# Two-stream cross-attention on one core: one subtraction moved behind two maxima, four weight subtractions moved to GpSimd

## Chip, cores and metric

One core of one Trainium2 chip runs the whole kernel. The metric is the device time of that core in microseconds. In this document "us" is always microseconds, PE is TensorE (matmuls), DVE is VectorE, ACT is ScalarE, POOL is GpSimd and SP is SyncE, which only issues transfers.

## The reference

A cross-attention layer: 2 x 2048 tokens of 640 channels attend, in 20 heads of 32, to 77 context vectors each (the second, image part of the context is empty here), and the input is added back.

```python
q = _split_heads(hidden_states @ Wq.T, H)
k = _split_heads(text @ Wk.T, H)
v = _split_heads(text @ Wv.T, H)
out_text = _merge_heads(_attend(q, k, v, sm_scale))   # softmax(q k * sm_scale) v
out = out_text + IP_SCALE * out_ip
out = out @ Wo.T + bo
return out + residual
```

## The kernel before

**Tiles.** The 4096 tokens are cut into NB = 8 blocks `t` of 512, the 640 channels into G = 5 groups `g` of 128, and each group holds 4 heads. The unit of work is a step (t, g), forty in all. Every engine runs its own program over the same steps, in its own fixed order: `run(engine, step, ...)` calls `step(t, g)` for all of them, the middle blocks in a hardware loop. The engines meet only at semaphores.

**Precision.** Each operand of a large product is split in two: a rounded high part (`x_hi`, `wq_hi`, `p_hi`, `attn_hi`) and the low rest (`x_lo`, ...). Three matmuls (hi·hi, lo·hi, hi·lo) make one product. The high part is an ACT copy or exponential. The low part is a subtraction of two tensors in SBUF, and these subtractions are divided between DVE and POOL: of the five chunks of x and of attn DVE has chunks 1 and 3 (`DVE_CHUNKS`), POOL 0, 2 and 4; of the four heads' probabilities DVE has head 0, POOL 1, 2 and 3.

**A step on PE** (`step`, L828): `values` of the step before (ps_pv, ps_den, L729 and L734), scores of heads 0 and 1 (ps_s, L722), `max_scores` tiles 0 and 1 of the next step (ps_m, L708), two chunks of an output projection (ps_o, L676), `max_scores` 2 and 3, scores 2, two more chunks, scores 3, `transpose_max` (ps_m, L713), the last chunk, and the query projection `project_q` of the step after the next (ps_q, L676, fifteen matmuls). `max_scores` has two buffers, so tiles 2 and 3 wait for DVE's maxima 0 and 1 (`max_done`, L704); `transpose_max` waits for all four (L712). `values` waits for `norm_done` (L740), the `normalise` that DVE made in the step before.

**A step on DVE** (`step`, L592): in the steps where x is split, `x_low` of chunk 1; then the maxima 0 and 1 (L534), `p_low` of head 0 (L541), the maxima 2 and 3, `x_low` of chunk 3, `invert_den` (two transposes and a reciprocal, L547 to L551), `normalise` (L561), `finish_out` (L580), and, once ACT has rounded q, `q_low` (L527).

**A step on POOL** (L341): `x_low` of chunks 0 and 2, `p_low` of head 1, `x_low` of chunk 4, `p_low` of heads 2 and 3. **On ACT** (L447): `x_high` of chunks 0 to 2, the two exponentials (p_f, p_hi) of heads 0 and 1, `x_high` of 3 and 4, heads 2 and 3 with `copy_max` between them, then `q_high`.

**Where x is split.** `x_split_at` gives block t + 1 at g = 3 of the blocks t = 1 to 6, so six steps of the forty split x. In this trace they lie one in every 50 us; block 0 and block 1 of x are split elsewhere.

**Start-up.** Until step (1, 0) PE runs `fill`, which also makes v (`project_v`, `transpose_v`). In it ACT rounds and DVE subtracts one chunk of wq a step (`query_group`: chunks 1 to 4 in the steps (-1, 3), (-1, 4), (0, 0), (0, 1)), each behind `q_high` and `q_low` of its step. Chunk 0 is made ahead of the steps. wo is rounded by ACT and subtracted by POOL (`wo_low`), its chunks 0 and 1 at the end of step (0, 1).

Of the kernel before, what the change touches and what calls it, by code (L numbers as in the profile page):

```python
# [18 lines left out]
def xattn_kernel(nc, x, ctx, wq, wk, wv, wo, bo, out):  # L19
# [63 lines left out]
    def query_group(t, g):  # L83

        return (nth(t, g) + 3,) if isinstance(t, int) and -2 <= nth(t, g) < G - 3 else ()
# [54 lines left out]
    with ExitStack() as stack:  # L140
# [159 lines left out]
        @block.gpsimd  # L300
        def _(pool):
            nc.gpsimd.memset(ident[:, :], 0.0).then_inc(zero_done, 1)
            pool.wait_ge(zero_done, 1)
            nc.gpsimd.affine_select(out=ident[:, :], in_=ident[:, :], compare_op=ALU.not_equal, fill=1.0,
                                    base=0, pattern=[[-1, P]], channel_multiplier=1).then_inc(ident_done, 1)
            pool.wait_ge(ident_done, 1)
            nc.gpsimd.memset(k_packed[:, :, :, :].bitcast(F32), -1.0).then_inc(const_done, 1)
            pool.wait_ge(const_done, 1)
            for i in range(RS):
                nc.gpsimd.memset(q_packed[:, i, :, :].bitcast(F32), 0.0).then_inc(q_cleared, 1)  # L310
            nc.gpsimd.memset(ones[:, :], 1.0).then_inc(const_done, 1)

            def x_low(t, chunks):
                for c in chunks:
                    pool.wait_ge(xhi_done, G * t + c + 1)
                    nc.gpsimd.tensor_tensor(x_lo[:, c, :], x_f[:, c, :], x_hi[:, c, :].bitcast(F32),  # L316
                                            ALU.subtract).then_inc(xlo_pool, 1)

            def p_low(t, g, i):

                pool.wait_ge(phi_done, HG * nth(t, g) + i + 1)
                pool.wait_ge(pf_done, HG * nth(t, g) + i + 1)
                if exists(shift(t, g, -1)[0]):
                    pool.wait_ge(pv_done, nth(t, g))
                nc.gpsimd.tensor_tensor(p_lo[:, i, :], p_f[:, i, :], p_hi[:, i, :],  # L325
                                        ALU.subtract).then_inc(plo_pool, 1)

            def attn_low(t, chunks):
                for c in chunks:
                    pool.wait_ge(ahi_done, G * t + c + 1)  # L330
                    nc.gpsimd.tensor_tensor(attn_lo[:, c, :], attn[:, c, :], attn_hi[:, c, :].bitcast(F32),
                                            ALU.subtract).then_inc(alo_pool, 1)

            x_low(0, POOL_CHUNKS)

            def wo_low(c):
                pool.wait_ge(wo_hi_done, c + 1)
                nc.gpsimd.tensor_tensor(wo_lo[:, c, :], wo_sb[:, c, :], wo_hi[:, c, :].bitcast(F32),
                                        ALU.subtract).then_inc(wo_lo_done, 1)

            def step(t, g):  # L341
                xt, (at, chunks) = x_split_at(t, g), attn_split_at(t, g)
                mine = [c for c in POOL_CHUNKS if c in chunks]
                if xt is not None:
                    x_low(xt, POOL_CHUNKS[:2])
                if exists(t):
                    p_low(t, g, 1)
                if xt is not None:
                    x_low(xt, POOL_CHUNKS[2:])
                attn_low(at, mine[:1])  # L350
                if exists(t):
                    p_low(t, g, 2)
                    p_low(t, g, 3)
                attn_low(at, mine[1:])
                if isinstance(t, int) and (t, g) == (0, 2):
                    x_low(1, POOL_CHUNKS)
                for c in wo_chunks(*shift(t, g, -1)):
                    wo_low(c)

            run(pool, step, *LOOP)  # L360

        @block.scalar
        def _(act):
# [12 lines left out]
            def diagonal_k(b, heads):  # L376
                act.wait_ge(mask_done, 1)
                act.wait_ge(khi_done, G)
                for i in heads:
                    nc.scalar.mul(k_diag[:, :, b, L * i:L * (i + 1)],  # L380
                                  k_hi[:, :, L * b:L * (b + 1)].bitcast(F32),
                                  head_mask[:, i:i + 1]).then_inc(diag_done, 1)

            def w_high(w_in, w_sb, w_hi, done, chunks):
                for c in chunks:
                    act.wait_ge(w_in[c], 16)
                    nc.scalar.copy(w_hi[:, c, :], w_sb[:, c, :]).then_inc(done, 1)
# [55 lines left out]
            x_high(0, range(G))  # L443
            start_k()
            diagonal_k(0, range(HG))

            def step(t, g):  # L447
                xt, (at, chunks) = x_split_at(t, g), attn_split_at(t, g)
                if xt is not None:
                    x_high(xt, range(0, 3))  # L450
                if exists(t):
                    exponentials(t, g, 0)
                    exponentials(t, g, 1)
                for tile in out_tiles(*shift(t, g, -1)):
                    store(*tile)
                if xt is not None:
                    x_high(xt, range(3, G))
                attn_high(at, [c for c in (0, 1) if c in chunks])
                if exists(t):
                    exponentials(t, g, 2)  # L460
                for v in value_group(t, g):
                    v_high(v)
                if exists(shift(t, g, 1)[0]):
                    copy_max(*shift(t, g, 1))
                if exists(t):
                    exponentials(t, g, 3)
                attn_high(at, [c for c in (2, 3) if c in chunks])
                for tile in out_tiles(*shift(t, g, 1)):
                    load_residual(*tile)
                attn_high(at, [c for c in (4,) if c in chunks])  # L470
                if exists(shift(t, g, 2)[0]):
                    q_high(*shift(t, g, 2))
                if isinstance(t, int) and (t, g) == (0, 2):
                    x_high(1, range(G))
                w_high(wq_in, wq_sb, wq_hi, wq_hi_done, query_group(t, g))
                if isinstance(t, int) and t == 0 and g <= 1:
                    diagonal_k(1, range(HG // 2 * g, HG // 2 * (g + 1)))
                w_high(wo_in, wo_sb, wo_hi, wo_hi_done, wo_chunks(*shift(t, g, -1)))
# [9 lines left out]
        def _(dve):  # L488
# [30 lines left out]
            def x_low(t, chunks):  # L519
                for c in chunks:  # L520
                    dve.wait_ge(xhi_done, G * t + c + 1)
                    nc.vector.tensor_tensor(x_lo[:, c, :], x_f[:, c, :], x_hi[:, c, :].bitcast(F32),
                                            ALU.subtract).then_inc(xlo_dve, 1)
# [68 lines left out]
            def step(t, g):  # L592
                xt, (at, chunks) = x_split_at(t, g), attn_split_at(t, g)
                last_t, last_g = shift(t, g, -1)
                if isinstance(t, int) and t == NB:
                    attn_low(at, 3)
                if xt is not None:
                    x_low(xt, DVE_CHUNKS[:1])
                for v in value_group(t, g):
                    scale_v(v)  # L600
                if exists(shift(t, g, 1)[0]):
                    reduce_max(*shift(t, g, 1), 0)
                    reduce_max(*shift(t, g, 1), 1)
                if exists(t):
                    p_low(t, g, 0)
                if exists(shift(t, g, 1)[0]):
                    reduce_max(*shift(t, g, 1), 2)
                    reduce_max(*shift(t, g, 1), 3)
                if xt is not None:
                    x_low(xt, DVE_CHUNKS[1:])  # L610
                for v in value_group(t, g):
                    v_low(v)
                if exists(last_t):
                    invert_den(last_t, last_g)
                    normalise(last_t, last_g)
                for tile in out_tiles(t, g):
                    finish_out(*tile)
                if 1 in chunks:
                    attn_low(at, 1)
                if exists(shift(t, g, 2)[0]):  # L620
                    q_low(*shift(t, g, 2))
                if 1 in chunks and 3 in chunks:
                    attn_low(at, 3)
                wq_low(query_group(t, g))
                if isinstance(t, int) and (t, g) == (0, 2):
                    x_low(1, DVE_CHUNKS)

# [290 lines left out]
```

## Time and profile before

| | us |
|---|---|
| median of 3 runs (lowest to highest) | 444.74 (444.53 to 446.11) |
| profiled execution | 445.5 |
| its span, first to last instruction | 443.7 |
| PE busy | 432.1 (97%) |
| DVE busy | 314.3 (71%) |
| ACT busy | 250.7 (57%) |
| POOL busy | 228.2 (51%) |

The granted TensorE clock was 0.995 over the span. Starts of matmuls in a row are some 0.23 us apart while each is recorded as 0.39 us, so matmuls overlap and a busy share of 97% does not say that nothing is lost: losses are read from the starts. A row of a timeline gives the start, the duration (of all, where several equal instructions in a row are merged), the engine, the line, the operation with its output and inputs, and in brackets how long the engine had been idle before it and who ended that.

### The profile page before, as it was taken

How to read it: one execution, taken by the hardware profiler on the slowest of the kernel's cores; microseconds unless marked ns; L12 is line 12 of the kernel's file. 1: busy time of each engine (PE TensorE's matmuls, PEld its weight loads, DVE VectorE, ACT ScalarE, POOL GpSimd, SP SyncE). 2: the span in 40 equal slices, each digit the busy share in tenths (PEclk: the TensorE clock that was granted, in tenths of full speed). 3: DMA queues.
4: the chain of work that ended last, by engine and by line, in shares of the span. 5: the costliest groups of instructions: out<-in, count | busy, mean ns of one | idle time of the engine just before them, and what ended most of it. 6: DMA issues, size and time to landing. Idle time of an engine off the chain costs nothing.

```text
span 443.7 us, 8269 instructions
## 1 busy us (share of the span) xinstructions
PE 432.1 (97%) x2538; PEld 313.7 (71%) x2538; DVE 314.3 (71%) x509; ACT 250.7 (57%) x509; POOL 228.2 (51%) x184
## 2 busy tenths in 40 slices
PE   8989989899999999999999999999999999999996
PEld 6967665576777767776777766777777766777675
DVE  0465896877869586967869586967869586966663
ACT  1728876846565464756565464756565464755510
POOL 7403796836546373636546373636546373634440
PEclk9999989999999999999999999999999999999999
DMA  8995433535344534445344534455345443445203
GB/s 286 398 394 161 160 101 127 192 123 189 121 143 164 178 136 145 173 180 195 120 144 160 178 139 144 169 182 194 123 143 166 154 157 120 148 154 177 73 24 120
DMA packets 39615, 72.70 MB, mean 164 GB/s; under 512 B 5024, under 2 KB 6176, under 8 KB 39584
## 3 DMA queue, kind: packets, MB, share of 16 engines
q1 hardware_dynamic: 28784, 52.62, 33.2%
q10 hardware_dynamic: 10800, 19.67, 13.9%
q8 instruction: 19, 0.31, 0.3%
q14 instruction: 12, 0.10, 0.1%
HBM read 28.81 MB, written 10.49 MB: 89 GB/s over the span
## 4 chain that ended last, share of the span: by engine, by line
PE 91%; DVE 3%; ACT 2%; issue 1%; DMA 1%; POOL 1%; DVEq 0%; ACTq 0%; POOLq 0%
PE ps_q L676 30%; PE ps_o L676 26%; PE ps_s L722 9%; PE ps_pv L729 6%; PE ps_m L708 6%; PE ps_den L734 4%; PE ps_m L773 1%; DMA q_packed<-mxT 1%; PE ps_s L647 1%; PE ps_m L713 1%; PE ps_o L660 1%; PE ps_q L773 1%; ACT p_f L415 1%; PE ps_q L639 1%; DVE x_f L573 1%
## 5 line engine op out<-in xcount | busy, mean ns | idle before, releaser
L325 POOL TENSOR_TENSOR p_lo<-p_f,p_hi 77x512 f16<-77x512 f32 x120 | 147.7, 1236 | 169.6 <-ACT p_hi L419 169.6
L415 ACT ACTIVATE p_f<-ps_s 77x512 f32<-77x512 f32 x160 | 95.0, 593 | 47.4 <-PE ps_s L722 47.4
L419 ACT ACTIVATE p_hi<-ps_s 77x512 f16<-77x512 f32 x160 | 93.9, 587 | 1.0 <-PE ps_den L734 0.8
L534 DVE TENSOR_REDUCE mx<-ps_m 128x4 f32<-128x308 f32 x160 | 68.8, 471 | 18.0 <-PE ps_m L708 17.5
L676 PE MATMUL ps_q<-x_hi,wq_hi 128*128 128x512 f32 x200 | 79.9, 399 | 0.0
L676 PE MATMUL ps_q<-x_hi,wq_lo 128*128 128x512 f32 x200 | 78.5, 393 | 0.0
L676 PE MATMUL ps_q<-x_lo,wq_hi 128*128 128x512 f32 x200 | 78.5, 392 | 0.0
L527 DVE TENSOR_TENSOR q_lo<-ps_q,q_hi 128x512 fp32r<-128x512 f32 x40 | 27.6, 690 | 68.7 <-ACT q_hi L398 68.7
L398 ACT CAST q_hi<-ps_q 128x512 fp32r<-128x512 f32 x40 | 23.4, 585 | 91.8 <-PE ps_q L676 91.8
L676 PE MATMUL ps_o<-attn_hi,wo_hi 128*128 128x512 f32 x170 | 69.5, 409 | 0.0
L676 PE MATMUL ps_o<-attn_lo,wo_hi 128*128 128x512 f32 x170 | 66.9, 394 | 0.0
L676 PE MATMUL ps_o<-attn_hi,wo_lo 128*128 128x512 f32 x170 | 66.9, 394 | 0.0
L722 PE MATMUL ps_s<-q_packed,k_packed 128*77 128x512 f32 x160 | 59.2, 413 | 1.8 <-DMA q_packed<-mxT 1.4
L316 POOL TENSOR_TENSOR x_lo<-x_f,x_hi 128x512 fp32r<-128x512 f32 x24 | 35.0, 1473 | 22.7 <-ACT x_hi L369 22.7
L676 PEld LDWEIGHTS ps_q<-x_hi,wq_hi 128*128 128x128 f32 x200 | 37.9, 190 | 9.6 <-issue 1.6
L708 PE MATMUL ps_m<-k_diag,q_hi 128*128 128x308 f32 x160 | 41.7, 327 | 2.4 <-DVE mx L534 2.2
L676 PEld LDWEIGHTS ps_q<-x_lo,wq_hi 128*128 128x128 f32 x200 | 37.8, 189 | 8.2
L676 PEld LDWEIGHTS ps_q<-x_hi,wq_lo 128*128 128x128 f32 x200 | 37.9, 189 | 7.8
L708 PEld LDWEIGHTS ps_m<-k_diag,q_hi 128*128 128x128 f32 x160 | 29.6, 188 | 18.3 <-DVE mx L534 11.2
L676 PEld LDWEIGHTS ps_o<-attn_hi,wo_hi 128*128 128x128 f32 x170 | 32.0, 188 | 7.8
L676 PEld LDWEIGHTS ps_o<-attn_lo,wo_hi 128*128 128x128 f32 x170 | 31.9, 188 | 7.2
L676 PEld LDWEIGHTS ps_o<-attn_hi,wo_lo 128*128 128x128 f32 x170 | 32.1, 189 | 4.5
(105 smaller groups left out, 602.5 us busy)
## 6 DMA issues: line engine op xcount, KB each, us to landing
q_packed<-q_hi SPq DMA_DIRECT2D x80, 256.0 KB, 2.5
x_f<-in_x SPq DMA_DIRECT2D x40, 256.0 KB, 3.1
q_packed<-q_lo SPq DMA_DIRECT2D x40, 256.0 KB, 3.2
x_res<-in_x ACTq DMA_DIRECT2D x35, 256.0 KB, 2.8
out<-out_sb ACTq DMA_DIRECT2D x35, 256.0 KB, 2.6
wk_sb<-in_wk SPq DMA_DIRECT2D x8, 320.0 KB, 5.2
wv_sb<-in_wv SPq DMA_DIRECT2D x5, 512.0 KB, 10.9
wq_sb<-in_wq SPq DMA_DIRECT2D x5, 320.0 KB, 9.0
```

Of the source, the lines that this page charges most:

```text
L316: nc.gpsimd.tensor_tensor(x_lo[:, c, :], x_f[:, c, :], x_hi[:, c, :].bitcast(F32), ALU.subtract).then_inc(xlo_pool, 1)
L325: nc.gpsimd.tensor_tensor(p_lo[:, i, :], p_f[:, i, :], p_hi[:, i, :], ALU.subtract).then_inc(plo_pool, 1)
L398: nc.scalar.copy(q_hi[:, g % RS, :], ps_q[:, :]).then_inc(qhi_done, 1)
L415: nc.scalar.activation(p_f[:, i, :], ps_s[i % 2][0:L, :], ACT.Exp, scale=SCALE).then_inc(pf_done, 1)
L419: nc.scalar.activation(p_hi[:, i, :], ps_s[i % 2][0:L, :], ACT.Exp, scale=SCALE).then_inc(phi_done, 1)
L527: nc.vector.tensor_tensor(q_lo[:, g % RS, :], ps_q[:, :], q_hi[:, g % RS, :].bitcast(F32), ALU.subtract).then_inc(qlo_done, 1)
L534: nc.vector.tensor_reduce(mx[:, g % RS, :, tt], ps_m[tt % 2][:, 0:HG * L].rearrange("p (h k) -> p h k", k=L), AX_X, ALU.max).then_inc(max_ ...
L676: last = nc.tensor.matmul(ps[:, :], w[:, k, P * c:P * (c + 1)], a[:, c, :], start=(c == 0 and n == 0), stop=(c == G - 1 and n == 2))
L708: nc.tensor.matmul(ps_m[tt % 2][:, 0:HG * L], q_hi[:, g % RS, P * tt:P * (tt + 1)], k_diag[:, g, b, :], start=True, stop=True).then_inc(ms ...
L722: nc.tensor.matmul(ps_s[i % 2][0:L, :], k_packed[:, i, g, L * b:L * (b + 1)], q_packed[:, g % RS, i, :], start=True, stop=True).then_inc(s ...
L729: nc.tensor.matmul(ps_pv[D * i:D * (i + 1), :], v[:, b, P * g + D * i:P * g + D * (i + 1)], p[:, i, :], tile_position=(0, D * i), **flags)
L734: last = nc.tensor.matmul(ps_den[D * i:D * (i + 1), :], ones[:, :], p[:, i, :], tile_position=(0, D * i), **flags)
```

## The change

On DVE `x_low` of the first of its chunks (chunk 1) moves from ahead of the maxima 0 and 1 to behind them, still ahead of `p_low`. DVE's `wq_low` of chunks 1 to 4 is taken out of its steps; POOL makes these chunks with a `wq_low` of its own, at the start of the same steps. ACT rounds each of these chunks one step earlier (chunk 1 ahead of the steps). Chunk 0 stays with DVE.

```diff
@@ POOL
+            def wq_low(c):
+                pool.wait_ge(wq_hi_done, c + 1)
+                pool.wait_ge(wq_lo_done, c)
+                nc.gpsimd.tensor_tensor(wq_lo[:, c, :], wq_sb[:, c, :], wq_hi[:, c, :].bitcast(F32),
+                                        ALU.subtract).then_inc(wq_lo_done, 1)
@@ POOL, step
                 mine = [c for c in POOL_CHUNKS if c in chunks]
+                for c in query_group(t, g):
+                    wq_low(c)
                 if xt is not None:
                     x_low(xt, POOL_CHUNKS[:2])
@@ ACT
             diagonal_k(0, range(HG))
+            w_high(wq_in, wq_sb, wq_hi, wq_hi_done, (1,))
@@ ACT, step
-                w_high(wq_in, wq_sb, wq_hi, wq_hi_done, query_group(t, g))
+                w_high(wq_in, wq_sb, wq_hi, wq_hi_done, query_group(*shift(t, g, 1)))
@@ DVE, step
-                if xt is not None:
-                    x_low(xt, DVE_CHUNKS[:1])
                 for v in value_group(t, g):
                     scale_v(v)
                 if exists(shift(t, g, 1)[0]):
                     reduce_max(*shift(t, g, 1), 0)
                     reduce_max(*shift(t, g, 1), 1)
+                if xt is not None:
+                    x_low(xt, DVE_CHUNKS[:1])
                 if exists(t):
                     p_low(t, g, 0)
@@ DVE, step
                     attn_low(at, 3)
-                wq_low(query_group(t, g))
                 if isinstance(t, int) and (t, g) == (0, 2):
```

## Rows read from the trace of the kernel before

**Rows 1.** Busy time by stretch: a step without an x split, one with.

```profile
core 0: us, PE busy (x) PEld busy (x) DVE busy (x) ACT busy (x) POOL busy (x), PEclk, DMA share, GB/s
192.44:202.27 9.83, 9.83 (x61) 7.19 (x60) 6.21 (x12) 4.94 (x12) 3.49 (x4) 1.00 0.44 161
202.27:212.62 10.35, 10.32 (x60) 7.17 (x60) 7.14 (x10) 7.33 (x17) 6.89 (x6) 1.00 0.53 180
```

**Rows 2.** Timeline of PE in a step with a split (start, duration).

```profile
207.34 0.45 PE L708 MATMUL ps_m<-k_diag,q_hi 128*128 128x308 f32 x2
...
208.77 0.40 PE L676 MATMUL ps_o<-attn_lo,wo_hi 128*128 128x512 f32 x1
209.20 0.79 PE L708 MATMUL ps_m<-k_diag,q_hi 128*128 128x308 f32 x2
...
211.65 0.27 PE L713 MATMUL ps_m<-ident,mx 128*16 128x128 f32 x1
...
215.97 0.40 PE L729 MATMUL ps_pv<-p_hi,v_hi 77*32 77x512 f16 x4
```

**Rows 3.** Timeline of DVE in the same step.

```profile
207.39 1.37 DVE L522 TENSOR_TENSOR x_lo<-x_f,x_hi 128x512 fp32r<-128x512 f32 x1 [0.35 <-ACT x_hi L369]
208.68 0.85 DVE L534 TENSOR_REDUCE mx<-ps_m 128x4 f32<-128x308 f32 x2
209.45 0.99 DVE L541 TENSOR_TENSOR p_lo<-p_f,p_hi 77x512 f16<-77x512 f32 x1
210.37 0.85 DVE L534 TENSOR_REDUCE mx<-ps_m 128x4 f32<-128x308 f32 x2
211.14 2.12 DVE L522 TENSOR_TENSOR x_lo<-x_f,x_hi 128x512 fp32r<-128x512 f32 x1
...
215.05 0.75 DVE L561 SCALAR_TENSOR_TENSOR attn<-ps_pv,v_scale,rden 128x512 f32<-128x512 f32 x1
```

**Rows 4.** Timeline of POOL in the same step.

```profile
206.91 2.99 POOL L316 TENSOR_TENSOR x_lo<-x_f,x_hi 128x512 fp32r<-128x512 f32 x2 [2.83 <-ACT x_hi L369]
209.89 1.58 POOL L325 TENSOR_TENSOR p_lo<-p_f,p_hi 77x512 f16<-77x512 f32 x1
211.44 1.28 POOL L316 TENSOR_TENSOR x_lo<-x_f,x_hi 128x512 fp32r<-128x512 f32 x1
```

**Rows 5.** Timeline of ACT in the same step.

```profile
209.22 0.60 ACT L419 ACTIVATE p_hi<-ps_s 77x512 f16<-77x512 f32 x1
209.69 1.15 ACT L369 CAST x_hi<-x_f 128x512 fp32r<-128x512 f32 x2
```

**Rows 6.** Timelines of POOL and DVE: subtractions that met no other, and one that did.

```profile
199.59 1.16 POOL L325 TENSOR_TENSOR p_lo<-p_f,p_hi 77x512 f16<-77x512 f32 x1 [5.33 <-ACT p_hi L419]
...
233.50 3.80 DVE L566 TENSOR_TENSOR attn_lo<-attn,attn_hi 128x512 fp32r<-128x512 f32 x1
...
237.83 0.68 DVE L566 TENSOR_TENSOR attn_lo<-attn,attn_hi 128x512 fp32r<-128x512 f32 x1
```

**Rows 7.** Timelines of POOL and DVE in start-up, subtractions of x's block 1.

```profile
58.61 2.97 POOL L316 TENSOR_TENSOR x_lo<-x_f,x_hi 128x512 fp32r<-128x512 f32 x2 [0.81 <-ACT x_hi L369]
...
59.08 3.04 DVE L522 TENSOR_TENSOR x_lo<-x_f,x_hi 128x512 fp32r<-128x512 f32 x2 [0.34 <-ACT x_hi L369]
```

**Rows 8.** Timelines of ACT, POOL, DVE and PE in start-up step (0, 2).

```profile
48.12 0.73 ACT L387 CAST wq_hi<-wq_sb 128x640 fp32r<-128x640 f32 x1
...
50.57 3.07 POOL L338 TENSOR_TENSOR wo_lo<-wo_sb,wo_hi 128x640 fp32r<-128x640 f32 x2 [2.58 <-ACT wo_hi L387]
...
52.32 1.88 DVE L541 TENSOR_TENSOR p_lo<-p_f,p_hi 77x512 f16<-77x512 f32 x1 [0.68 <-ACT p_hi L419]
...
54.06 0.39 PE L676 MATMUL ps_q<-x_lo,wq_hi 128*128 128x512 f32 x1
55.02 0.28 PE L713 MATMUL ps_m<-ident,mx 128*16 128x128 f32 x1 [0.58 <-DVE mx L534]
```

**Rows 9.** ACT in step (-1, 3); landing of wq's chunk 1 (us from issue).

```profile
21.30 0.59 ACT L398 CAST q_hi<-ps_q 128x512 fp32r<-128x512 f32 x1 [0.90 <-PE ps_q L676]
...
wq_sb<-in_wq SPq DMA_DIRECT2D x1, 320.0 KB, 7.8
```

## The prediction

> **What bounds the kernel now.** I read the busy time by stretch first, then the timelines of one step engine by engine. In a step without an x split PE is busy 9.83 us of 9.83; a step with a split takes 10.35 [rows 1], 0.52 us more, though PE has the same work in it. So PE sets the pace, and what a change of the other engines can win is only the time by which PE starts late. The place is seen in PE's timeline: the last ps_o matmul starts at 208.77, the next start would be due some 0.23 later, at 209.00, but the third ps_m starts at 209.20 and the pair takes 0.79 instead of the 0.45 of the first pair [rows 2]. Both ps_m buffers were still being reduced: DVE began with x_lo at 207.39 and held it for 1.37, so the first maxima ran from 208.68 to 209.53, though their ps_m had been there since 207.79 [rows 2, 3]. That is the stall which the change aims at. There are six such steps, so its whole worth is 6 x 0.52 = 3.1 us.
>
> **A second clock in the same step.** Every subtraction here reads two tensors of SBUF, on DVE and on POOL, and the rows show that two of them don't run side by side. Alone, DVE's takes 0.68 [rows 6]. In the split step it took 1.37, 0.99 and 2.12, and where POOL had a row of them 3.80 [rows 3, 6]. Where the rows show both, its end lies 0.55 behind an end of a POOL subtraction: 209.45 + 0.99 = 210.44 against POOL's pair, which ends at 209.90 [rows 3, 4]; 211.14 + 2.12 = 213.26 against 211.44 + 1.28 = 212.72. The other way round POOL's p_lo, 1.16 alone [rows 6], took 1.58 and ended at 211.47, 1.03 behind DVE's 210.44. So one waits for the whole of the other's instruction, and I use two rules from these rows: DVE ends 0.55 behind the POOL instruction that it waits for, POOL's p_lo 1.03 behind DVE's.
>
> **Part 1, the moved x_lo, step by step.** The maxima 0 and 1 now start when ps_m is there, at 207.7 to 207.8, and with their 0.85 end at about 208.6 [rows 2, 3]. PE's tiles 2 and 3 go at 209.00 without a wait: the old stall is gone. The transpose, which PE reached at 211.65, is then due 0.55 earlier, at 211.10. What is late next is what stands ahead of it on DVE: x_lo, p_lo and the maxima 2 and 3, and only then may PE transpose. The x_lo, ready at 208.6, meets POOL's second x_lo. In the trace of before that one was held up by DVE; without that it runs from 208.2 (DVE's x_lo end 208.76 less 0.55) for 1.25 to 1.28 [rows 3, 4], to about 209.46. DVE's x_lo therefore ends at 209.46 + 0.55 = 210.01. That is the price of the new place: 1.25 us later than the 208.76 of before, where the maxima came only 1.0 earlier. Next DVE's p_lo wants to run, and POOL's p_lo of head 1 becomes ready at nearly the same moment: ACT ends p_hi at 209.82 [rows 5] and POOL follows some 0.07 later, at 209.90. Who goes first decides the case.
>
> If DVE goes first, its p_lo ends 0.6 after the x_lo, at 210.60 (an end 0.68 behind a start that overlaps its forerunner by 0.08, as 211.14 against 210.37 + 0.85 shows [rows 3]). The maxima end 0.78 later, as before (211.22 against 210.44 [rows 3]), at 211.38, and PE transposes at 211.43, 0.22 earlier than before [rows 2]. Then x_lo of chunk 3: POOL's p_lo ends at 210.60 + 1.03 = 211.63, its x_lo of chunk 4 comes next as it did before [rows 4], to 212.88, and DVE's ends at 213.43 where it was 213.26. Everything behind it moves by 0.17: normalise, which ended at 215.80 [rows 3], ends at 215.97. PE's values wait for it. They started at 215.97 [rows 2] and would be due at 215.75, but can't start before about 216.02. So the 0.52 won at ps_m is lost to 0.30 at the transpose and to the rest at the values: **0.05 us slower in each split step, 0.3 in all.** The new wait has taken the place of the old one.
>
> Costed at nothing: the tail of the step on ACT and SP, since both only follow PE (mxT is copied behind the transpose, and its transfer is needed a whole step's start later), and DVE's finish_out and q_lo, behind which DVE idles for 0.35 [rows 3]; if that cover were gone it would be 0.17 a step.
>
> **Part 2, wq's low part on POOL.** DVE loses four subtractions of some 0.8 us. They lay right behind q_lo while PE was still making v, and the work that follows on DVE waits for PE's v projection, so their going gives nothing by itself. POOL gains four of 3.07 / 2 = 1.54 us [rows 8] in steps in which it has nothing else until the probabilities come. Bounds: nothing if its idle time covers them, 1.54 for each that doesn't fit; POOL's first p_lo of a step follows more than 2 us after each, so I take nothing. ACT's cast of chunk 1 now stands ahead of the first q_hi. ACT idled 0.90 ahead of it and the cast takes 0.73 [rows 8, 9], and the chunk lands 7.8 after its issue in the first eleven us [rows 9], so it fits; if it did not, up to 0.7 us would be lost once.
>
> The casts' shift helps in one place. At 48.12 ACT cast wq's chunk 4 for 0.73 [rows 8]; this cast now lies a step earlier, so the casts of wo behind it, and POOL's wo_lo pair that waits for them, come up to 0.7 earlier. In step (0, 2) that pair ran from 50.57 to 53.64 and DVE's p_lo, wanted at 52.32, waited for it until 54.20 [rows 8]. With the pair's end near 53.0 DVE's p_lo ends near 53.6, and the maxima and PE's transpose come 0.6 earlier: it started at 55.02 where PE was due at 54.06 + 0.23 = 54.29, a stall of 0.73 [rows 8]. I take **0.6 us faster**, once (0 to 0.7).
>
> **The sum.** The profiled execution took 445.5 with a span of 443.7; the median of the runs is 444.74, and the differences are applied to it. 444.74 + 0.3 - 0.6 = 444.4.
>
> **A rule of the skill against the trace.** The subtractions' ends show the blocking by themselves [rows 3, 4, 6]. By the Trainium skill, page SBUF — State Buffer, section Who interferes with whom, a DVE instruction with two SBUF inputs contends with a POOL instruction that reads SBUF, and "issue order, not op shape, decides who blocks". The trace agrees in size. Taken literally for the tie at 209.90 that rule favours POOL, whose instruction would issue first by 0.02 us; that is the first rival.
>
> **Rivals.** (1) *POOL wins the tie*, in every split step. For it: at start-up two DVE x_lo stood back to back and POOL's second x_lo got in between, since DVE's pair ended at 62.12, 0.54 behind the end of POOL's pair at 61.58 [rows 7]; DVE doesn't keep its place from one instruction to the next. Against: there POOL had long been waiting, here it becomes ready only 0.1 ahead of DVE's end, and the 0.13 by which POOL's p_lo is shorter behind a DVE instruction (1.16 against 1.03) is work that it must do first. Price: POOL's p_lo runs to 211.06, DVE's ends at 211.61, the maxima at 212.39, the transpose comes at 212.44 instead of 211.65, **0.79 us later** in each of six steps. 4.7 - 0.6 gives 448.8. It decides as soon as POOL's p_lo has its turn before the end of DVE's x_lo: slower than before. (2) *And POOL's x_lo of chunk 4 goes too.* Its input is ready at 210.84 [rows 5], ahead of 211.06. DVE waits until 212.3, the transpose comes at 213.7, 2.0 late: 444.7 + 12.2 - 0.6 = 456.3. POOL did pass DVE so at 211.44 [rows 4] and twice in the 3.80 [rows 6], but there DVE had asked when POOL's next was ready, or nearly; here it has asked 0.8 before. (3) *DVE wins the tie and also gets x_lo of chunk 3 in ahead of POOL's chunk 4.* Then normalise is no limit and 0.22 a step is kept: 444.7 - 1.3 - 0.6 = 442.8. (4) *The subtractions don't get in each other's way at the new place*: the full stall goes, 444.7 - 3.1 - 0.6 = 441.0. That the start-up part does nothing, a change that doesn't do what it says, adds 0.6 to each.
>
> **How the numbers follow.** DVE first, with the values' limit, 0.44: 444.4, with own range 443.9 to 445.2. POOL first 0.30: 448.8. A mixture of both over the six steps, since a tie of 0.02 us may fall either way, 0.08: 445 to 448. Both POOL instructions first 0.06: 456.3. Rival 3, 0.06: 442.8. Rival 4, 0.06: 441.0. The range from 442.5 to 449.3 holds all but rivals 2 and 4. Half a per cent, about what a measurement can tell from no change, is 2.2 us: faster, below 442.5, is rival 4 and a little of rival 3, 0.08; slower, above 447.0, is rivals 1 and 2 and half of the mixture, 0.40; the same 0.52.
>
> **What would show it.** In the split steps the third ps_m starts 0.23 behind ps_o, and DVE's order is mx x2, x_lo, p_lo, mx x2. Right, if x_lo ends near 210.0 on the clock of these rows and p_lo 0.6 behind it, POOL's p_lo takes about 1.7, and the split steps last about 10.4. Rival 1 shows as a DVE p_lo of some 1.7 and split steps of 11.1; rival 2 as 12.4. In start-up POOL's wo_lo pair starts near 49.9, and the transpose of step (0, 2) near 54.4. The prediction is wrong if the x_lo does not wait for POOL's second one, or if PE's values start without waiting for normalise.

## The result and the profile after

The changed kernel takes 449.78 us (448.78 to 451.35, four runs) against 444.63 us, a ratio of 1.0112 (95% interval 1.0075 to 1.0148). Measured once more, on another chip with the kernel before, it gave 449.16 against 444.86, 1.0092 (1.0061 to 1.0122). It is slower by about one per cent, 4 to 5 us.

Lines of the changed file stand up to nine further down than those of before: the maxima are L543 there, DVE's `x_low` L531, its `p_low` L550, the projections L684, `transpose_max` L721. POOL's `x_low` and `p_low` keep L316 and L325.

Busy time by stretch of the kernel after, from one PE transpose to the next: an ordinary step, the split step, an ordinary one (the columns are those of [rows 1]).

```profile
core 0: us, PE busy (x) PEld busy (x) DVE busy (x) ACT busy (x) POOL busy (x), PEclk, DMA share, GB/s
191.44:201.28 9.84, 9.84 (x61) 7.20 (x59) 6.16 (x12) 4.94 (x10) 3.50 (x4) 1.00 0.47 161
201.28:212.42 11.14, 9.96 (x60) 7.11 (x59) 7.57 (x11) 7.33 (x15) 7.25 (x6) 1.00 0.48 167
212.42:222.23 9.81, 9.81 (x60) 7.21 (x60) 7.73 (x14) 4.94 (x10) 4.33 (x5) 1.00 0.38 134
```

The split step was 10.35 [rows 1] and is 11.14, and PE is busy for 9.96 of it: the rest is one gap. The other steps are as they were. PE's timeline of the kernel after shows where the gap is:

```profile
208.75 0.39 PE L684 MATMUL ps_o<-attn_lo,wo_hi 128*128 128x512 f32 x1
208.98 0.44 PE L716 MATMUL ps_m<-k_diag,q_hi 128*128 128x308 f32 x2
...
210.85 0.39 PE L730 MATMUL ps_s<-q_packed,k_packed 128*77 128x512 f32 x1
212.42 0.28 PE L721 MATMUL ps_m<-ident,mx 128*16 128x128 f32 x1 [1.18 <-DVE mx L543]
```

The old stall is gone: the third ps_m starts 0.23 behind ps_o, and the pair takes 0.44 instead of 0.79 [rows 2]. But the transpose, due at 211.08, starts at 212.42, having waited for the maxima. DVE and POOL of the kernel after in the same step, answering to [rows 3, 4]:

```profile
207.66 0.87 DVE L543 TENSOR_REDUCE mx<-ps_m 128x4 f32<-128x308 f32 x2 [0.64 <-PE ps_m L716]
208.44 1.55 DVE L531 TENSOR_TENSOR x_lo<-x_f,x_hi 128x512 fp32r<-128x512 f32 x1
209.92 1.67 DVE L550 TENSOR_TENSOR p_lo<-p_f,p_hi 77x512 f16<-77x512 f32 x1
211.51 0.85 DVE L543 TENSOR_REDUCE mx<-ps_m 128x4 f32<-128x308 f32 x2
212.29 0.97 DVE L531 TENSOR_TENSOR x_lo<-x_f,x_hi 128x512 fp32r<-128x512 f32 x1
```

```profile
206.89 2.56 POOL L316 TENSOR_TENSOR x_lo<-x_f,x_hi 128x512 fp32r<-128x512 f32 x2 [2.82 <-ACT x_hi L377]
209.87 1.17 POOL L325 TENSOR_TENSOR p_lo<-p_f,p_hi 77x512 f16<-77x512 f32 x1 [0.43 <-ACT p_hi L427]
211.00 1.71 POOL L316 TENSOR_TENSOR x_lo<-x_f,x_hi 128x512 fp32r<-128x512 f32 x1
```

DVE's x_lo waits for POOL's second one (end 209.45) and ends 0.54 behind it, at 209.99. DVE's p_lo then takes 1.67: POOL's p_lo was issued at 209.87, ran undisturbed for 1.17 to 211.04, and DVE's ended 0.55 behind it, at 211.59. POOL's next x_lo, at 1.71, was the one that waited: DVE came in ahead of it.

The six intervals with a split are 11.12 to 11.16 in the kernel after and 10.35 to 10.38 before: 0.77 each, 4.6 in all. The order is the same in all six: POOL's p_lo starts 0.11 to 0.12 ahead of the end of DVE's x_lo and goes first. The start-up step (0, 2) went the other way:

```profile
49.82 3.08 POOL L344 TENSOR_TENSOR wo_lo<-wo_sb,wo_hi 128x640 fp32r<-128x640 f32 x2 [1.92 <-ACT wo_hi L395]
52.18 1.25 DVE L550 TENSOR_TENSOR p_lo<-p_f,p_hi 77x512 f16<-77x512 f32 x1 [0.68 <-ACT p_hi L427]
...
54.27 0.28 PE L721 MATMUL ps_m<-ident,mx 128*16 128x128 f32 x1
```

POOL's wo_lo pair starts 0.75 earlier than in [rows 8], DVE's p_lo takes 1.25 instead of 1.88, and PE transposes with no wait shown. The interval up to this transpose is 9.15 in the kernel after (45.12 to 54.27) and was 9.79, a gain of 0.64.

So the traces give 4.6 - 0.64 = 4.0. The spans differ by 3.1 only (446.8 and 443.7), mainly because the profiled execution of before had a stretch at the lower clock in start-up and that of after had none. Kernel before, the interval that it fell in and the stretch itself, then the same interval of the kernel after:

```profile
55.02:66.78 11.76, 10.49 (x62) 7.52 (x63) 10.72 (x19) 8.30 (x17) 10.65 (x9) 0.89 0.28 95
64.20:67.60 3.40, 3.40 (x11) 2.56 (x11) 3.17 (x6) 1.70 (x5) 3.24 (x3) 0.50 0.02 5
```

```profile
54.27:65.39 11.12, 9.48 (x64) 6.63 (x63) 10.41 (x18) 8.37 (x18) 10.02 (x8) 1.00 0.31 102
```

In those 3.4 us the granted clock was 0.50 (1.2 of 2.4 GHz), and the interval is 0.64 longer. That the clock is the cause and not the changed start-up is seen in run 1 below, `move_only`, which has the start-up of the kernel before: at full clock throughout, this interval took 11.11 there. Differences are therefore read below from intervals at full clock, and not from spans.

### The profile page after: what moved, and what is told of

Same layout as the page of the kernel before. It is cut to its first block, busy times and chain, and to the rows that moved or that the text cites. A ratio compares the mean times of both kernels' runs of the same rounds, so it can differ in the third digit from the quotient of the medians.

```text
span 446.8 us, 8273 instructions
## 1 busy us (share of the span) xinstructions
PE 428.3 (96%) x2538; PEld 311.0 (70%) x2538; DVE 309.1 (69%) x505; ACT 250.6 (56%) x509; POOL 231.7 (52%) x188
## 4 chain that ended last, share of the span: by engine, by line
PE 84%; DVE 7%; issue 3%; ACT 2%; DMA 2%; POOL 1%; DVEq 0%; ACTq 0%; POOLq 0%
PE ps_q L684 29%; PE ps_o L684 22%; PE ps_s L730 8%; PE ps_pv L737 6%; PE ps_m L716 5%; PE ps_den L742 4%; DVE mx L543 2%; DVE p_lo L550 2%; DMA q_packed<-mxT 2%; PE ps_o L668 1%; DVE x_lo L531 1%; PE ps_m L721 1%; PE ps_m L781 1%; PE ps_s L655 1%; PE ps_q L781 1%
## 5 line engine op out<-in xcount | busy, mean ns | idle before, releaser
L325 POOL TENSOR_TENSOR p_lo<-p_f,p_hi 77x512 f16<-77x512 f32 x120 | 145.0, 1213 | 161.7 <-ACT p_hi L427 161.7
L543 DVE TENSOR_REDUCE mx<-ps_m 128x4 f32<-128x308 f32 x160 | 68.9, 471 | 22.1 <-PE ps_m L716 21.6
L684 PE MATMUL ps_q<-x_hi,wq_hi 128*128 128x512 f32 x200 | 79.3, 397 | 0.1
L684 PE MATMUL ps_q<-x_lo,wq_hi 128*128 128x512 f32 x200 | 78.2, 391 | 0.0
L684 PE MATMUL ps_q<-x_hi,wq_lo 128*128 128x512 f32 x200 | 78.0, 390 | 0.0
L684 PE MATMUL ps_o<-attn_hi,wo_hi 128*128 128x512 f32 x170 | 69.4, 408 | 0.0
L684 PE MATMUL ps_o<-attn_hi,wo_lo 128*128 128x512 f32 x170 | 66.9, 394 | 0.0
L684 PE MATMUL ps_o<-attn_lo,wo_hi 128*128 128x512 f32 x170 | 66.9, 393 | 0.0
L316 POOL TENSOR_TENSOR x_lo<-x_f,x_hi 128x512 fp32r<-128x512 f32 x24 | 35.0, 1474 | 23.1 <-ACT x_hi L377 23.1
L684 PEld LDWEIGHTS ps_q<-x_hi,wq_hi 128*128 128x128 f32 x200 | 37.6, 188 | 9.8 <-issue 1.9
L684 PEld LDWEIGHTS ps_q<-x_lo,wq_hi 128*128 128x128 f32 x200 | 37.5, 188 | 8.2
L684 PEld LDWEIGHTS ps_q<-x_hi,wq_lo 128*128 128x128 f32 x200 | 37.6, 188 | 7.7
L716 PE MATMUL ps_m<-k_diag,q_hi 128*128 128x308 f32 x160 | 39.6, 319 | 2.3 <-DVE mx L543 2.3
L550 DVE TENSOR_TENSOR p_lo<-p_f,p_hi 77x512 f16<-77x512 f32 x40 | 35.1, 877 | 4.8 <-ACT p_hi L427 4.8
L684 PEld LDWEIGHTS ps_o<-attn_lo,wo_hi 128*128 128x128 f32 x170 | 31.9, 188 | 7.2
L684 PEld LDWEIGHTS ps_o<-attn_hi,wo_hi 128*128 128x128 f32 x170 | 32.0, 188 | 6.9
```

Source lines behind the costliest of these rows:

```text
L543: nc.vector.tensor_reduce(mx[:, g % RS, :, tt], ps_m[tt % 2][:, 0:HG * L].rearrange("p (h k) -> p h k", k=L), AX_X, ALU.max).then_inc(max_ ...
L550: nc.vector.tensor_tensor(p_lo[:, i, :], p_f[:, i, :], p_hi[:, i, :], ALU.subtract).then_inc(plo_dve, 1)
L684: last = nc.tensor.matmul(ps[:, :], w[:, k, P * c:P * (c + 1)], a[:, c, :], start=(c == 0 and n == 0), stop=(c == G - 1 and n == 2))
L716: nc.tensor.matmul(ps_m[tt % 2][:, 0:HG * L], q_hi[:, g % RS, P * tt:P * (tt + 1)], k_diag[:, g, b, :], start=True, stop=True).then_inc(ms ...
```

## The experiments

All are compared with the kernel before on the same chip. "Block" is five intervals between PE's transposes around t = 3, one of them with a split: 49.98 in the kernel before (from 192.44), 50.74 in the kernel after (from 191.44).

**1 and 2. The two parts alone.** `move_only` has the moved x_lo and nothing of wq; `wq_only` is the changed kernel with the x_lo put back.

```diff
 # wq_only, DVE step, against the changed kernel
+                if xt is not None:
+                    x_low(xt, DVE_CHUNKS[:1])
                 for v in value_group(t, g):
...
                     reduce_max(*shift(t, g, 1), 1)
-                if xt is not None:
-                    x_low(xt, DVE_CHUNKS[:1])
```

> Only DVE's x_lo of chunk 1 is moved behind the maxima 0 and 1; wq stays as it was. Theory (the tie goes to POOL: DVE's p_lo waits for POOL's whole p_lo): split steps of 11.14 us as in the changed kernel against 10.37, so 6 x 0.77 = 4.6 slower than before, ratio near 1.010, and start-up as before. Rival (the wq part, with its new POOL work and the earlier casts, costs some of the loss): less than 4.6 slower, ratio at or under 1.005.

> Only wq's low part moves to POOL and its casts a step earlier; DVE's x_lo stays ahead of the maxima. Theory: 0.65 us faster than before, from the transpose of step (0, 2) that comes 0.7 earlier, ratio 0.9985; split steps stay at 10.37. Rival (this part costs something): ratio above 1.000.

`move_only`: 449.28, ratio 1.0102 (1.0083 to 1.0121). `wq_only`: 444.21, ratio 0.9980 (0.9962 to 0.9997). The split step of each, move_only first:

```profile
202.11:213.24 11.13, 9.96 (x60) 7.11 (x59) 7.56 (x11) 7.32 (x15) 7.25 (x6) 1.00 0.49 167
```

```profile
202.67:213.06 10.39, 10.36 (x60) 7.16 (x59) 7.11 (x11) 7.19 (x15) 6.93 (x6) 1.00 0.52 179
```

The whole loss is the moved x_lo's, and the wq part is a small gain. Its interval up to the transpose of step (0, 2) is 9.15, against 9.79 before and 9.77 in move_only.

**3 and 4. Tipping the tie.** The changed kernel gets one tiny ACT copy in the split steps, so that POOL's p_lo of head 1 becomes ready a little later. This adds work and takes none away.

```diff
             def exponentials(t, g, i):
...
+                if x_split_at(t, g) is not None and i == 1:
+                    nc.scalar.copy(nudge[:, :], head_mask[:, :])
                 if exists(shift(t, g, -1)[0]):
                     act.wait_ge(pv_done, nth(t, g))
                 nc.scalar.activation(p_hi[:, i, :], ps_s[i % 2][0:L, :], ACT.Exp,
```

In `tie_act` the 16-byte tile `nudge` was allocated between x_f and x_hi, so x_f stayed where it was and x_hi and all tiles behind it moved 16 bytes further:

> The changed kernel with one tiny ACT copy (128 x 4) ahead of the second exponential of head 1 in the split steps, so that POOL's p_lo of head 1 becomes ready some 0.2 us later. It does more work and nothing else. Theory (the tie decides): DVE's p_lo takes 0.68 instead of 1.67, the transpose comes some 1.0 earlier than in the changed kernel, values then wait for normalise; split steps near 10.4, total 444.0 to 445.0, that is 4 us faster than the changed kernel. Rival (POOL gets its turn behind every DVE subtraction, tie or not): DVE's p_lo stays at 1.7 or grows, split steps of 11.1 or more, total 449 or more.

447.67, ratio 1.0059 (1.0041 to 1.0078), where 444.0 to 445.0 was expected. The transpose did come earlier (split steps of 10.20 to 10.23), but every ordinary step was 9.93 instead of 9.84, with ps_q matmuls 0.233 apart instead of 0.227. So the tile went to the end of the allocation, in `tie_act_end`:

> The changed kernel with the same tiny ACT copy in the split steps, but its 16-byte tile now stands behind all other tiles, so that no other tile's address moves. In the run with the tile in front the ps_q matmuls started 0.233 apart instead of 0.227 in every step. Theory (the tie decides, and the other loss of that run came from the moved addresses): ordinary steps of 9.84 again, the five steps of a block together 50.05 where the changed kernel has 50.8 and the kernel before 50.03; total near 444.2, 4.5 under the changed kernel. Rival (the copy itself slows the steps): the five steps stay at 50.4, total 447.5.

444.77, ratio 1.0003 (0.9990 to 1.0015), some 4.4 us under `move_only` and the second measurement of the changed kernel. Its DVE and POOL:

```profile
207.16 1.55 DVE L534 TENSOR_TENSOR x_lo<-x_f,x_hi 128x512 fp32r<-128x512 f32 x1
208.63 0.68 DVE L553 TENSOR_TENSOR p_lo<-p_f,p_hi 77x512 f16<-77x512 f32 x1
209.23 0.85 DVE L546 TENSOR_REDUCE mx<-ps_m 128x4 f32<-128x308 f32 x2
210.01 2.14 DVE L534 TENSOR_TENSOR x_lo<-x_f,x_hi 128x512 fp32r<-128x512 f32 x1
```

```profile
208.69 1.65 POOL L326 TENSOR_TENSOR p_lo<-p_f,p_hi 77x512 f16<-77x512 f32 x1 [0.53 <-ACT p_hi L430]
210.30 1.29 POOL L317 TENSOR_TENSOR x_lo<-x_f,x_hi 128x512 fp32r<-128x512 f32 x1
```

The copy itself took 0.19, of which 0.1 delayed the exponential. In the kernel after POOL's p_lo was issued 0.12 ahead of the end of DVE's x_lo and 0.05 ahead of DVE's p_lo, and went first. Here it was issued 0.02 ahead of that end (208.69 against 208.71) and 0.06 behind DVE's p_lo, and had to wait: 1.65 for POOL, 0.68 for DVE. All six split steps of this trace and of `tie_act` went this way. A shift of 0.1 us of one engine decides 1.0 us at the transpose (11.14 against 10.14) and 0.6 over the block (50.74 against 50.13). The forecast, with DVE first, was 49.98 + 0.05; the rest of the time won at the transpose comes back as a wait for normalise in the next interval, which grew to 10.19:

```profile
200.00:210.14 10.14, 9.96 (x60) 7.10 (x59) 6.58 (x11) 6.95 (x16) 6.14 (x5) 1.00 0.55 183
210.14:220.33 10.19, 9.92 (x59) 7.27 (x60) 8.85 (x14) 5.26 (x11) 5.51 (x6) 1.00 0.37 129
```

```profile
214.83 0.40 PE L740 MATMUL ps_pv<-p_hi,v_hi 77*32 77x512 f16 x4 [0.27 <-DVE attn L573]
```

**5. Taking POOL's holding time away.** `short_pool` computes only 8 of the 512 columns of x's low part in POOL's chunks 0, 2 and 4, from block 2 on; the rest of these chunks is left out.

```diff
+                    n = TB if isinstance(t, int) and t < 2 else 8
-                    nc.gpsimd.tensor_tensor(x_lo[:, c, :], x_f[:, c, :], x_hi[:, c, :].bitcast(F32),
+                    nc.gpsimd.tensor_tensor(x_lo[:, c, 0:n], x_f[:, c, 0:n], x_hi[:, c, 0:n].bitcast(F32),
```

> The changed kernel with POOL's x_lo cut to its first 8 of 512 columns from block 2 on (the rest of x's low part in chunks 0, 2 and 4 isn't computed), so that POOL holds the shared access for a short time only. Theory (the loss is waiting for POOL's instructions): DVE's moved x_lo takes 0.68, p_lo 0.7, no stall of PE at ps_m, the transpose or values: split steps 9.84, the block of five 49.5, total 440.8. Rival (the loss lies in DVE's own amount of work at this place): split steps stay above 10.3, total above 444.

441.23, ratio 0.9919 (0.9902 to 0.9935). With DVE's order and work as in the changed kernel, the split step is 9.80 and the moved x_lo and the p_lo take 0.68 each:

```profile
206.10 0.68 DVE L532 TENSOR_TENSOR x_lo<-x_f,x_hi 128x512 fp32r<-128x512 f32 x1
206.69 0.68 DVE L551 TENSOR_TENSOR p_lo<-p_f,p_hi 77x512 f16<-77x512 f32 x1
```

So DVE's amount of work at this place costs nothing; waiting for POOL does. The run is 3.6 us under the kernel before: about what the change could have won at most, since the columns left out are work that a full kernel has to do.

**6. POOL's order.** `pool_order` puts POOL's x_lo of chunk 4 ahead of its p_lo of head 1.

```diff
-                if exists(t):
-                    p_low(t, g, 1)
                 if xt is not None:
                     x_low(xt, POOL_CHUNKS[2:])
+                if exists(t):
+                    p_low(t, g, 1)
```

> The changed kernel with POOL's x_lo of chunk 4 ahead of its p_lo of head 1 in the split steps. POOL is then idle until chunk 4 is rounded, near 210.9 on the clock of the trace of before. Theory: DVE's p_lo takes 0.68 and its maxima end near 211.38, PE transposes near 211.43, DVE's x_lo of chunk 3 waits for one POOL instruction only and normalise ends near 215.3, so it no longer limits values: split steps of 10.15, total 442.7, 0.4% under before. Rival (POOL's late p_lo of heads 2 and 3 holds up values or the next exponentials): split steps of 10.4 or more, total 444 or more.

444.20, ratio 0.9983 (0.9970 to 0.9996). The split intervals are 10.12 to 10.16 as expected, but the next are 9.96 to 10.11, and most of the gain is gone. The rival was right that POOL's late p_lo would hold up the values, though not with its split steps of 10.4. Why they were so late was not foreseen:

```profile
210.42 0.67 DVE L531 TENSOR_TENSOR x_lo<-x_f,x_hi 128x512 fp32r<-128x512 f32 x1
```

```profile
210.03 2.23 POOL L316 TENSOR_TENSOR x_lo<-x_f,x_hi 128x512 fp32r<-128x512 f32 x1 [1.45 <-ACT x_hi L377]
212.21 3.40 POOL L325 TENSOR_TENSOR p_lo<-p_f,p_hi 77x512 f16<-77x512 f32 x3
```

POOL's x_lo is recorded from 210.03, with no subtraction of DVE running, and yet DVE's, issued at 210.42, ran undisturbed and POOL's ended 1.16 behind it. So POOL's three p_lo ended at 215.61. The values with the high part had begun at 214.88, and those that read p_lo could start at 215.76 only, 0.44 behind the last one before them where 0.22 is usual:

```profile
215.32 0.39 PE L742 MATMUL ps_den<-p_hi,ones 77*32 77x512 f16 x4
215.76 0.40 PE L737 MATMUL ps_pv<-p_lo,v_hi 77*32 77x512 f16 x4
```

**7. DVE's order.** `dve_late` puts both of DVE's x_lo behind the maxima 2 and 3.

```diff
-                if xt is not None:
-                    x_low(xt, DVE_CHUNKS[:1])
                 if exists(t):
                     p_low(t, g, 0)
...
                 if xt is not None:
-                    x_low(xt, DVE_CHUNKS[1:])
+                    x_low(xt, DVE_CHUNKS)
```

> The changed kernel with both of DVE's x_lo behind the maxima 2 and 3 (order: maxima 0 and 1, p_lo, maxima 2 and 3, x_lo of chunks 1 and 3). Theory: DVE's p_lo asks near 208.9 on the clock of before, ends 0.55 behind POOL's second x_lo, near 210.0, maxima at 210.8, so PE transposes without a wait; both x_lo then wait for POOL one after the other, normalise ends near 215.8 and values wait for it: the block of five 49.9 against 50.03, total 443.3. Rival (the late x_lo holds up the query projection's chunk 1 or 3): the block of five above 50.3, total above 445.

444.85, ratio 0.9990 (0.9978 to 1.0001), no difference. PE no longer waits in the split interval, but in the next one:

```profile
202.92:212.72 9.80, 9.80 (x60) 7.19 (x59) 5.89 (x10) 6.61 (x14) 5.90 (x6) 1.00 0.56 190
212.72:224.24 11.52, 10.36 (x60) 7.10 (x59) 10.13 (x15) 5.51 (x12) 5.68 (x5) 1.00 0.33 115
```

Two of the six such intervals were 11.5, this one among them, and the others 10.25 to 10.35. The difference is who went first at the end of POOL's p_lo (212.69). Here POOL's x_lo of chunk 4 did, though DVE's had been issued 0.32 before it, and normalise, for which PE's values waited, came late:

```profile
212.33 3.73 DVE L531 TENSOR_TENSOR x_lo<-x_f,x_hi 128x512 fp32r<-128x512 f32 x2
```

```profile
212.65 1.29 POOL L316 TENSOR_TENSOR x_lo<-x_f,x_hi 128x512 fp32r<-128x512 f32 x1
```

```profile
218.74 0.40 PE L735 MATMUL ps_pv<-p_hi,v_hi 77*32 77x512 f16 x4 [0.91 <-DVE attn L570]
```

In the other four, with the same instructions issued at the same distances within 0.01, DVE went first: its first x_lo took 0.90, and the block took 49.9 to 50.0, where 49.9 was expected. So the place of the wait was as expected, and its size in four blocks of six.

**8. A version that beats both.** `balanced` gives x's chunk 0 to DVE, which idles 0.64 ahead of the first maxima, and spreads POOL's instructions over its gaps.

```diff
+    X_DVE, X_POOL = (0, 1, 3), (2, 4)
 # DVE, split step: x_low 0, maxima 0 and 1, x_low 1, p_low 0, maxima 2 and 3, x_low 3
+                if xt is not None:
+                    x_low(xt, X_DVE[:1])
                 for v in value_group(t, g):
...
 # POOL, split step: x_low 2, p_low 1, p_low 2, x_low 4, p_low 3
-                    x_low(xt, POOL_CHUNKS[:2])
+                    x_low(xt, X_POOL[:1])
```

> From the changed kernel: x's chunk 0 goes from POOL to DVE, ahead of the maxima 0 and 1, where DVE is idle; chunk 1 stays behind them; POOL's order in the split step is x_lo 2, p_lo 1, p_lo 2, x_lo 4, p_lo 3. Theory (each DVE subtraction costs 0.55 of the shared access, each of POOL's 1.2, and what counts is who stands at the access when): DVE's x_lo of chunk 0 ends near 207.6 on the clock of before, no tie at 209.9 (DVE's p_lo is already running), x_lo of chunk 3 finds POOL idle near 211.3: split steps of 9.84 to 9.9, total 440.8 to 441.5, 0.8% under before. Rival (DVE's added subtraction or POOL's late x_lo 4 or p_lo 3 stall PE): split steps of 10.2 or more, total 443.5 or more.

441.15 (440.84 to 441.45), ratio 0.9909 (0.9896 to 0.9922): 3.9 us under the kernel before, some 8 under the changed one. The split step is 9.93 (9.84 to 9.9 was expected), and the next one 9.83. Some 0.5 of the gain lies in start-up, where chunk 0 of block 1 went to DVE as well: the interval of 11.12 in the kernel after is 10.63 here.

```profile
198.82:208.75 9.93, 9.93 (x61) 7.11 (x59) 6.96 (x12) 6.74 (x15) 4.78 (x4) 1.00 0.55 187
208.75:218.58 9.83, 9.83 (x60) 7.21 (x60) 7.63 (x14) 5.36 (x12) 5.08 (x6) 1.00 0.38 134
```

```profile
204.47 0.68 DVE L533 TENSOR_TENSOR x_lo<-x_f,x_hi 128x512 fp32r<-128x512 f32 x1
205.20 0.87 DVE L545 TENSOR_REDUCE mx<-ps_m 128x4 f32<-128x308 f32 x2
205.98 1.34 DVE L533 TENSOR_TENSOR x_lo<-x_f,x_hi 128x512 fp32r<-128x512 f32 x1
207.24 0.68 DVE L552 TENSOR_TENSOR p_lo<-p_f,p_hi 77x512 f16<-77x512 f32 x1
207.84 0.85 DVE L545 TENSOR_REDUCE mx<-ps_m 128x4 f32<-128x308 f32 x2
208.61 0.88 DVE L533 TENSOR_TENSOR x_lo<-x_f,x_hi 128x512 fp32r<-128x512 f32 x1
```

```profile
205.47 1.30 POOL L317 TENSOR_TENSOR x_lo<-x_f,x_hi 128x512 fp32r<-128x512 f32 x1 [3.87 <-ACT x_hi L379]
207.41 1.54 POOL L326 TENSOR_TENSOR p_lo<-p_f,p_hi 77x512 f16<-77x512 f32 x1 [0.64 <-ACT p_hi L429]
```

DVE's p_lo is issued at 207.24, before POOL's at 207.41, so there is no tie left. POOL waits for DVE once (p_lo, 1.54 against 1.16 alone), and DVE for POOL once for long (1.34 against 0.68) and once for 0.2. The run does not tell apart what chunk 0's move gave and what POOL's new order gave.

**9. The changed kernel again, and the address of x_f.** `after_again` is the changed kernel; `shift16` and `shift64` have an unused tile of that many bytes ahead of x_f and no instruction more.

```diff
+        x_f_offset = sb("x_f_offset", [P, 4], F32)   # 16 for shift64
         x_f = sb("x_f", [P, G, TB], F32)
```

> The changed kernel itself once more, on one chip with the kernel before. Its two parts alone gave ratios of 1.0102 and 0.9980, together 1.0082, while it gave 1.0112 in its own measurement. Theory (the parts add up; the rest was scatter of the runs, in which the granted TensorE clock differed): ratio 1.007 to 1.009, split steps 11.14 in the trace. Rival (the parts cost more together than apart): ratio 1.010 or more.

> The changed kernel with an unused 16-byte tile ahead of x_f, so that x_f and all tiles behind it lie 16 bytes further; no instruction is added. Theory (the address alone made ps_q matmuls slower in the run with ACT's tiny copy): ps_q matmuls start 0.233 apart, ordinary steps 9.93, total about 3.3 above the changed kernel. Rival (the copy did it): steps of 9.84, total as the changed kernel.

> The same with an unused tile of 64 bytes. Theory (what counts is the place within a block of 64 bytes): no cost, steps of 9.84, total as the changed kernel. Rival (any move of x_f costs): steps of 9.93.

`after_again`: 449.16, ratio 1.0092 (1.0061 to 1.0122), split intervals 11.12 to 11.16. The parts' product, 1.0082, lies in both intervals of the whole, so nothing shows that they cost more together; the measurement can't exclude some tenths of a per cent. `shift16`: 452.43, ratio 1.0168 (1.0135 to 1.0201); `shift64`: 449.86, ratio 1.0114 (1.0079 to 1.0149). An ordinary step of each, shift16 first:

```profile
191.47:201.40 9.93, 9.93 (x60) 7.19 (x59) 6.13 (x12) 4.94 (x10) 3.48 (x4) 1.00 0.45 159
```

```profile
222.95:232.80 9.85, 9.85 (x60) 7.19 (x59) 6.01 (x11) 5.64 (x12) 3.84 (x4) 1.00 0.48 161
```

Sixteen bytes cost 0.09 a step with no instruction added, sixty-four nearly none, in line with the 9.93 of `tie_act`. There x_f itself had not moved, so it is not needed for this: the cost comes with the place of x_hi or of a tile behind it.

## Why the prediction was wrong

**The old stall**, seen at ps_m and said to go: right. **The x_lo at its new place** was forecast to end at 210.01 and ended at 209.99. **The bounds of the tie** were right too: POOL ready at 209.90 (measured 209.87), DVE's p_lo from 209.93 (209.92). The lead of POOL's start over DVE's, which the prediction gives as 0.02, is 0.03 by its own figures and was 0.05.

**The step that failed is who goes first.** It was given to DVE with 0.44 against 0.30, on the argument that POOL's p_lo must first do 0.13 of its own work before it needs the access, so that 0.1 of lead was not enough. That 0.13 was worked out from ends (1.16 against 1.03), which show how long an instruction lasts behind another, not when it asks. The traces of the kernel after and of runs 3 and 4 measured it: a lead of 0.12 over the end of DVE's x_lo is enough for POOL, one of 0.02 is not. So DVE's p_lo, forecast to end 0.6 behind the x_lo, ended 1.60 behind it, and PE transposed 0.77 later than before instead of 0.22 earlier. The Trainium skill, page SBUF — State Buffer, section Who interferes with whom, has "issue order, not op shape, decides who blocks", and by the recorded starts that rule was right both times (209.87 against 209.92, POOL; 208.69 against 208.63, DVE). The prediction named it and gave it the smaller chance. It is not the whole rule: in `pool_order` DVE passed a POOL instruction issued 0.39 ahead of it, and in [rows 3, 4] POOL's x_lo at 211.44 went ahead of DVE's, issued at 211.14.

**The first rival** gave the size: 0.79 a step forecast, 0.77 measured, 448.8 for the kernel. Its further steps held as well: POOL's x_lo of chunk 4 let DVE pass (rival 2 fell), and normalise did not limit the values. **The forecast case** was right for the case it described: with the tie tipped, `tie_act_end` gave a block of 50.13 against 50.03 forecast, with the wait for normalise that the forecast names, and the same time as before within the scatter. Its split step is 10.14 and not the 10.4 of "What would show it": counted between transposes, the prediction's own 0.22 gives 10.13, and the loss lies in the next interval. So the mechanism, its place and the price of the first rival were right, the price of the forecast case was 0.1 a block too low, and a difference of 0.05 us between two engines was called the wrong way.

**Part 2** was forecast at 0.6 faster and gave 0.64 in the trace and, alone, 0.20% (0.03 to 0.38%). It came through the casts of wo, as said; the four subtractions taken from DVE gave nothing visible.

**The range** ended at 449.3, half a microsecond above the first rival, and the median was 449.78. It had no room for the scatter of the runs themselves: the four of the changed kernel span 2.6 us, with granted clocks from 0.991 to 1.000 over the execution. `after_again`, 449.16, lies inside it. Rival 4, the full stall gone, was right as a size: `short_pool` gave 441.2 where it had 441.0.

## What to carry to other kernels

When work of one engine is moved behind other work, look at what the second engine starts while it waits: here the x_lo started 1.05 later on its own engine, behind POOL's second subtraction instead of its first, and its end met the start of the next. Where two such instructions become ready within some 0.1 us, count the case as undecided and price both ways, or move one so that the order is plain. Removing a stall on the engine that bounds the kernel is worth only what the next wait in the same step leaves; the version that won moved work into idle time of the engine behind which the other waits less: DVE ends 0.55 behind POOL, POOL 1.0 to 1.2 behind DVE. That this is why it won is argued and not shown.

## What the runs showed of the hardware

- Two subtractions with both inputs in SBUF, on DVE and POOL, run one after the other in every run: DVE ends 0.55 behind the POOL instruction that it waits for, POOL's p_lo 1.03 behind DVE's (in the kernel before) and its x_lo 1.14 (before) to 1.16 (`pool_order`).
- At an end of DVE's, POOL's p_lo goes next if it was issued 0.12 before that end (six steps of the kernel after), not if 0.02 before (six steps each of `tie_act` and `tie_act_end`).
- Who goes next at an end of POOL's is not settled by these runs. DVE, issued 1.1 before that end, got in ahead of POOL's x_lo of chunk 4 in the kernel after; issued 0.33 before it, it did not in the kernel before [rows 3, 4]; in `dve_late`, issued 0.36 before it, it did in four steps and did not in two, where its x_lo pair took 3.73. A longer wait is no guarantee: in the 3.80 of [rows 6], asked for at 233.50, DVE was passed twice, by POOL's two attn_lo from 234.23 to 236.75. In `pool_order` DVE passed one already recorded as started.
- The place of x_hi and of the tiles behind it in a partition counts for matmuls: 16 bytes further made ps_q matmuls 0.233 apart instead of 0.227 (`tie_act`, `shift16`), 64 bytes further made an ordinary step 9.85 instead of 9.84 (`shift64`). Which of these tiles it is stays open.
- The TensorE clock was at its lower level for 3.4 us in start-up in some profiled executions, in that of before from 64.2, after a wait of PE of 1.3 us (from 62.3 to 63.6). The wait does not decide it alone: the trace of after has the same one (61.6 to 62.9) and full speed. It also stayed at full speed through the waits of 1.2 us in the split steps of after.
